# First attention of a four-stage kernel: q and k parts of each eight heads in their own 64 partitions and DRAM block, with row 0 written and loaded per block and its low parts made on VectorE

## The chip, the cores and the metric

One core of a Trainium2 chip. The metric is the device time of one execution in microseconds (us), median of several runs; the profile is of one execution of its own.

## What is computed

Four residual blocks run one after the other on x of shape (4, 1024, 128): an attention with a window of 64 keys, a gated linear attention with routing, an attention mixed with a recurrent state, and a mixture of experts. The change touches the first block alone:

```python
def _L0_attn_ref(x, Wq, Wk, Wv, Wo):          # x: layer-normed, 16 heads of 8 values
    q = (x @ Wq.T).reshape(b, s, 16, 8)
    k = (x @ Wk.T).reshape(b, s, 16, 8)
    v = (x @ Wv.T).reshape(b, s, 16, 8)
    attn = jnp.einsum('bqhd,bkhd->bhqk', q, k) / np.sqrt(8)
    allowed = (j <= i) & (j > i - 64)
    attn = softmax(jnp.where(allowed, attn, -jnp.inf))
    out = jnp.einsum('bhqk,bkhd->bqhd', attn, v).reshape(b, s, 128)
    return out @ Wo.T
x = x + _L0_attn_ref(_layernorm(x), ...)
```

## The kernel before, in words

A "row" is one of the four batch rows (b = 0 to 3) of 1024 positions. `window()` is the first attention. Every engine walks one list, `window_order()`, and does its own share of each item in that order; semaphores (named signals, `wait_ge`) join them. So an engine that waits in an item holds all its later items back.

For each row: `norm`, `log`, `root`, `tiles`, `turn` make the normed row and transpose it; `q` and `k` project it (TensorE, L496) into PSUM (128 partitions x 1024). To score in bf16 without losing the fp32 result, q and k are each split into three bf16 parts: the high part (ScalarE, L679), the rest in fp32 (VectorE, L612), the mid part (ScalarE, L684), and the low part (GpSimd, L828, `pool_low`). These parts lie in SBUF (`a_parts`), with one copy for q and one for k, so a row's parts may be made only when the row before has been read out.

SyncE writes the parts to DRAM (`a_scratch`, L748): each of the three parts goes to one, two or three of the six places of a stack (`PLACES`), 768, 512 and 256 KB for q, and the same sum for k in four DMAs. Then they are loaded back (L732, `load_half`) as stacks of 48 = 6 x 8 rows: one load has the four heads of a unit half `r` and goes to partitions 0-47 (r = 0) or 64-111 (r = 1). A unit (b, e) is eight heads of a row; e = 0, 1. Its four loads (q and k, r = 0 and 1) are 384 KB each. The loads `L` are issued by SyncE; those with r = 1 are issued by ScalarE (`L2`), but for unit (0, 0), where SyncE issues all four.

`M` (b, e, n) scores 128 queries for their maxima (TensorE, L475 the masks, L521 the products), and VectorE reduces them (L628). When the eight of a unit are done, GpSimd splits the negated maxima in three (L815 to L821), `S` transposes them (L530), ScalarE copies (L701), and SyncE puts them into rows 48-50 and 112-114 of the q stacks with six small DMAs (L763, the "shift rows"). `W` (b, e, m) then scores keys against queries (L475, L545), ScalarE exponentiates (L708), `V` weighs the values (L561), `D` and `E` add up (L718, L638). `M` items run seven ahead of `W`, which crosses units: in the list M(0,1,0) and M(0,1,1) stand ahead of S(0,0), and M(1,0,0) stands behind W(0,0,1).

At the start the list is: all of row 0's projection, its writes, `L` of (0,0), `L` of (0,1), values of row 0, norm and turn of row 1, `L2` of (0,1), `q` of row 1, M(0,0,0), `mid q` and `k` of row 1, three M, `mid k` of row 1, row 1's writes, four M, two M of (0,1), S(0,0), `L` of (1,0) and (1,1), `L2` of (1,0). Later rows' projections, writes and loads are spread over the steps of `W`: row 2's writes at steps 7 and 8, its first loads at 9, its first `L2` at 11; row 3 likewise 16 steps later.

Of the kernel before, what the change touches and what calls it, by code (L numbers as in the profile page):

```python
# [7 lines left out]
ALU = mybir.AluOpType  # L8
# [3 lines left out]
BF16 = mybir.dt.bfloat16  # L12

P = 128
BANK = 512
EPS = 1e-5
HEADS, HD = 16, 8
# [12 lines left out]
SPLIT = 3  # L30
# [85 lines left out]
def build(nc, x_in, packed, x_out, place, batches, T, known):  # L116
# [7 lines left out]
    with ctx:  # L124
# [7 lines left out]
        pe, dv, ac, gp, sp = (Queue(e) for e in (nc.tensor, nc.vector, nc.scalar, nc.gpsimd, nc.sync))  # L132
# [201 lines left out]
        a_scratch = {s: nc.dram_tensor(f"a_scratch_{s}", (batches, len(PARTS), P, T + P), BF16, kind="Internal").ap() for s in "qk"}  # L334
# [19 lines left out]
        def window_order():  # L354
# [7 lines left out]
                                 [("turn", b, 1)], [("q", b)], [("mid", b, "q"), ("k", b)], [("mid", b, "k")]]  # L362
# [16 lines left out]
            order = (flat(project(0)) + writes(0) + loads(0, 0) + loads(0, 1) + [("v", 0, 0), ("v", 0, 1)] + flat(second[:5])  # L379
# [43 lines left out]
        def window():  # L423
            s = "a"
# [165 lines left out]
            def dve_program():  # L590
                for ps in slots:
                    nc.vector.memset(ps[:, :], 0.0).then_inc(a_sums_cleared.up("all"), 1)
                for item in order:
# [13 lines left out]
                    elif kind in ("q", "k"):  # L607
                        b = item[1]
                        dv.wait_ge(a_split, (kind, b, "high"))
                        if b:  # L610
                            dv.wait_ge(a_low_made, (kind, b - 1))
                        nc.vector.tensor_tensor(a_rest[kind][:, :], ps[:, :], a_parts[kind][:, 0, :], ALU.subtract).then_inc(  # L612
                            a_rest_made.up((kind, b)), 1)
                    elif kind == "v":
# [46 lines left out]
            def act_program():  # L661
                for item in order:
# [11 lines left out]
                    elif kind in ("q", "k"):  # L674
                        b = item[1]
                        ac.wait_ge(a_projected, (kind, b))
                        if b:
                            ac.wait_ge(a_scratch_there[kind], b - 1)
# [7 lines left out]
                    elif kind == "L2":  # L686
# [4 lines left out]
                        ac.wait_ge(a_scratch_there[side], b)  # L691
# [38 lines left out]
            def load_half(engine, b, side, e, r):  # L730
                rows = a_scratch[side][b].rearrange("i (d r e p) t -> r e (i d) p t", r=2, e=2, d=HD)
                return engine.dma_start(a_stacks[side][b % 2][half(r, SCORE), SIDES * e:SIDES * (e + 1), :],  # L732
                                        rows[r, e][:, :, 0:T])

            def sp_program():
                for item in order:
                    kind = item[0]
                    if kind == "write":
                        _, b, side = item
                        for a in range(SPLIT):  # L740
                            if a < 2:
                                sp.wait_ge(a_split, (side, b, ("high", "mid")[a]))
                            else:
                                sp.wait_ge(a_low_made, (side, b))
                            for first, n, apart in PLACES[side][a]:
                                blocks = a_scratch[side][b].rearrange("i x t -> x i t")[
                                    :, first:first + (n - 1) * apart + 1:apart, 0:T]
                                nc.sync.dma_start(blocks, a_parts[side][:, a, :].unsqueeze(1).to_broadcast([P, n, T])).then_inc(  # L748
                                    a_scratch_there[side].up(b, 16), 16)
                    elif kind == "late":  # L750
                        sp_load_constants_late(a_staged)
                        for b in range(3, batches):
                            sp_load_x(b)
                        sp_load("b")
                    elif kind == "S":
                        _, b, e = item
                        u = unit(b, e)
                        sp.wait_ge(a_neg_T_made, (b, e))
                        for r in range(2):
                            for a in range(SPLIT):  # L760
                                row = 64 * r + SCORE + a
                                first = (r * SPLIT + a) * SIDES
                                nc.sync.dma_start(a_stacks["q"][b % 2][row:row + 1, SIDES * e:SIDES * (e + 1), :],  # L763
                                                  a_neg_T[u % 2][first:first + SIDES, :]).then_inc(
                                    a_shift_there[u % 2].up((b, e), 16), 16)
                    elif kind == "L":
                        _, b, side, e = item
                        sp.wait_ge(a_cleared, ("shift", b % 2))
                        if b >= 2:
                            sp.wait_ge(a_key_scored, ("W", b - 2, e, NT - 1))  # L770
                        sp.wait_ge(a_scratch_there[side], b)
                        for r in range(2 if (b, e) == (0, 0) else 1):
                            load_half(nc.sync, b, side, e, r).then_inc(stack_there[b % 2, e].up((s, b, e), 16), 16)
                        if item == ("L", 0, "k", 1):
                            sp_load_x(2)

            def pool_program():
# [13 lines left out]
                for side in "qk":  # L791
                    pool_low(side, 0)
# [30 lines left out]
            def pool_low(side, b):  # L823
                gp.wait_ge(a_split, (side, b, "mid"))
                gp.wait_ge(a_rest_made, (side, b))
                if b:
                    gp.wait_ge(a_scratch_there[side], b - 1)
# [1198 lines left out]
        def gla_first_pool():  # L2026

            gp.wait_ge(constants_made, "all")
            for side in "qk":
                gp.wait_ge(a_scratch_there[side], batches - 1)  # L2030
# [831 lines left out]
def weight_columns(i):  # L2862
# [11 lines left out]

    by_part = np.arange(P).reshape(-1, 2, HD).transpose(2, 1, 0).reshape(-1)
# [14 lines left out]
    for h in range(2):  # L2890
# [6 lines left out]
        "a_wq": i["L0_attn_Wq"].T[:, by_part], "a_wk": i["L0_attn_Wk"].T[:, by_part], "a_wv": i["L0_attn_Wv"].T,  # L2897
# [41 lines left out]
```

## Time and profile before

| | |
|---|---|
| median of 3 runs | 1802.07 us (1801.25 to 1804.1) |
| the profiled execution | 1806.19 us |
| its span, first to last instruction | 1804.9 us |
| mean granted TensorE clock | 0.951 of 2.4 GHz |
| busy: TensorE / VectorE / ScalarE / GpSimd | 1556.2 / 1275.3 / 1098.3 / 697.8 us |

The first attention fills about the first 280 us. A timeline row gives the start and the length in us, engine, line, operation, what it writes and reads, the count, and in brackets the idle time ahead of it and what ended that. SPq and ACTq are DMA issues of SyncE and ScalarE; a row of several goes from the first issue to the last and has their waits in it. "issue" as the releaser means that the profile shows nothing that the engine waited for.

### The profile page before, as it was taken

Reading aid. Unit: us, or ns where it says so; the run is one execution under the profiler, and the core shown is the slowest. Engines: PE = TensorE matmul, PEld = TensorE weight load, DVE = VectorE, ACT = ScalarE, POOL = GpSimd, SP = SyncE. Lnnn points to the kernel's source line nnn. Section 1 sums busy time; section 2 is a strip of 40 time slices with the busy share of each in tenths; the row PEclk is TensorE's granted clock in tenths of the full one; section 3 lists DMA queues with packets and bytes.
Section 4 is the critical chain, followed back from the end, with each engine's and each line's share of the span. In section 5 each row is a group of like instructions: output and inputs, shape, how many; then the busy total and the mean of one; then the engine's idle time right before and its main releaser. Section 6 shows DMA issues by size and latency. Waiting matters only on the chain. (4 is left out here: it accounts for less than half of the span.)

```text
span 1804.9 us, 45554 instructions
## 1 busy us (share of the span) xinstructions
PE 1556.2 (86%) x19648; PEld 998.5 (55%) x19648; DVE 1275.3 (71%) x2003; ACT 1098.3 (61%) x1641; POOL 697.8 (39%) x499
## 2 busy tenths in 40 slices
PE   3587897899999999999977778888788888899999
PEld 2354566787778778877863232433333343466565
DVE  4656644777777677768767868778777886655665
ACT  3255576777767777786752567677667767533331
POOL 4122300554255344534450556365465545411100
PEclk8789898999999999999997889999999999999999
DMA  7864200000000000000024274246237222223332
GB/s 176 196 165 113 47 5 12 2 2 2 2 2 2 2 1 2 2 1 2 32 88 99 52 212 98 63 133 142 56 107 167 66 64 72 67 71 94 95 96 76
DMA packets 54821, 121.17 MB, mean 67 GB/s; under 512 B 6124, under 2 KB 14468, under 8 KB 53020
## 3 DMA queue, kind: packets, MB, share of 16 engines
q1 hardware_dynamic: 51708, 112.74, 23.7%
q10 hardware_dynamic: 2912, 5.51, 1.8%
q8 instruction: 155, 2.54, 0.6%
q14 instruction: 46, 0.38, 0.1%
HBM read 85.70 MB, written 31.74 MB: 65 GB/s over the span
## 5 line engine op out<-in xcount | busy, mean ns | idle before, releaser
L1445 DVE TENSOR_REDUCE arena<-ring 128x2 f32<-128x1024 f32 (+2 forms) x320 | 342.1, 1110 | 87.9 <-PE ring L1302 62.1
L1545 ACT ACTIVATE arena<-ring 128x1024 f32<-128x1024 f32 (+1 forms) x320 | 291.3, 937 | 135.4 <-PE ring L1331 92.0
L1352 PE MATMUL accs<-arena 128*9 128x512 f32 (+3 forms) x1536 | 174.3, 528 | 3.8 <-ACT arena L1545 3.8
L2509 POOL TENSOR_TENSOR arena<-arena 128x1280 f32<-128x1280 f32 x28 | 65.3, 2332 | 287.0 <-PE accs L2270 231.7
L1295 PE MATMUL ring<-arena 48*128 48x512 bf16 (+3 forms) x768 | 128.8, 347 | 41.8 <-DVE arena L1445 21.1
L1324 PE MATMUL ring<-arena 51*128 51x512 bf16 (+3 forms) x768 | 125.0, 343 | 45.8 <-DVE arena L1445 25.1
L2501 POOL TENSOR_TENSOR arena<-arena 128x512 f32<-128x512 f32 x112 | 141.3, 1294 | 3.0 <-DVE arena L2311 3.0
L287 POOL TENSOR_SCALAR xn<-x,moments,rstd 128x128 f32<-128x128 f32 x80 | 65.0, 825 | 192.3 <-DVE rstd L258 178.3
L2782 ACT ACTIVATE arena<-ring 128x512 f32<-128x512 f32 x80 | 47.7, 596 | 134.8 <-PE ring L2651 132.7
L2494 POOL TENSOR_TENSOR arena<-arena 128x1024 f32<-128x1024 f32 x32 | 86.3, 2698 | 108.1 <-DVE arena L2368 108.1
L1718 POOL TENSOR_TENSOR arena<-arena 128x1024 f32<-128x1024 f32 x28 | 65.9, 2354 | 128.6 <-ACT arena L1558 104.5
L2742 DVE TENSOR_TENSOR arena<-arena,ring 128x512 f32<-128x512 f32 x80 | 54.9, 687 | 82.9 <-PE ring L2653 70.3
L1324 PEld LDWEIGHTS ring<-arena 51*128 51x128 bf16 x768 | 36.6, 95 | 137.9 <-DVE arena L1445 75.6
L2665 PEld LDWEIGHTS accs<-weights_large,arena 128*128 128x128 f32 x640 | 83.6, 193 | 37.9 <-issue 31.6
L1295 PEld LDWEIGHTS ring<-arena 48*128 48x128 bf16 x768 | 38.4, 96 | 110.3 <-DVE arena L1445 42.6
L2665 PE MATMUL accs<-weights_large,arena 128*128 128x128 f32 x640 | 85.3, 277 | 0.7 <-DVE arena L2748 0.7
L2454 ACT ACTIVATE arena<-arena 128x512 f32<-128x512 f32 x128 | 81.4, 707 | 0.0
L628 DVE TENSOR_REDUCE arena<-ring 128x8 f32<-128x1024 f32 x49 | 59.3, 1220 | 29.2 <-PE ring L521 29.0
L2246 PE MATMUL ring<-arena 128*64 128x256 f32 x512 | 76.0, 381 | 0.0
L1706 POOL TENSOR_TENSOR arena<-arena 128x1024 f32<-128x1024 f32 x32 | 75.5, 2360 | 0.1
L1455 DVE TENSOR_TENSOR_SCAN arena<-arena 128x1024 f32<-128x1024 f32 x32 | 73.8, 2306 | 2.3 <-POOL arena L1706 2.3
L2244 PEld LDWEIGHTS ring<-arena 128*64 128x64 f32 x512 | 36.1, 135 | 60.2 <-issue 30.6
(342 smaller groups left out, 4165.9 us busy)
## 6 DMA issues: line engine op xcount, KB each, us to landing
arena<-whole_k SPq DMA_DIRECT2D x32, 512.0 KB, 4.6
arena<-whole_q SPq DMA_DIRECT2D x32, 512.0 KB, 6.2
arena<-moe_scratch SPq DMA_DIRECT2D x128, 128.0 KB, 2.9
arena<-c_scratch_q SPq DMA_DIRECT2D x14, 384.0 KB, 9.3
arena<-c_scratch_k SPq DMA_DIRECT2D x14, 384.0 KB, 12.2
a_scratch_k<-arena SPq DMA_DIRECT2D x8, 512.0 KB, 4.2
c_scratch_k<-arena SPq DMA_DIRECT2D x8, 512.0 KB, 4.5
arena<-a_scratch_q SPq DMA_DIRECT2D x9, 384.0 KB, 7.2
```

Source lines behind the costliest of these rows:

```text
L1295: mm = nc.tensor.matmul(o[r], qs[half(r, SCORE), pair, n * P:(n + 1) * P], ks[half(r, SCORE), pair, a:c], start=True, stop=not diag)
L1324: mm = nc.tensor.matmul(o[r], ks[half(r, SHIFT), 2 * g + pair, j * P:(j + 1) * P], qs[half(r, SHIFT), 2 * g + pair, a:a + cols], start=Tru ...
L1352: mm = nc.tensor.matmul(acc[ci % 2][32 * h:32 * h + HD + 1, a - c * BANK:BANK], c_values[b % 2][:, j, r * HEADS // 2 + 2 * g + i, :], weig ...
L1445: nc.vector.tensor_reduce(dst, src, AX.X, ALU.max, negate=True).then_inc(c_max_taken.up(item), 1)
L1455: nc.vector.tensor_tensor_scan(sk[:, :], c_retain[:, j:j + 1].to_broadcast([P, T]), sk[:, :], 0.0, ALU.mult, ALU.add).then_inc(c_state_mad ...
L1545: nc.scalar.activation(view(c_probs[wi % 4]), view(ps), ACT.Exp).then_inc(c_weights_made.up(item), 1)
L1706: nc.gpsimd.tensor_tensor(sk[:, :], sk[:, :], c_vT[:, :], ALU.mult).then_inc(c_kv_made.up((b, j)), 1)
L2246: mm = nc.tensor.matmul(ps[r * GLA_D:(r + 1) * GLA_D, o + GLA_D:o + DENSE * GLA_D], k_nat[1][:, cols], v5[t % 2][:, 1:DENSE, cols], start= ...
L2454: nc.scalar.activation(v5[t % 2][:, 1 + r, :], v5[t % 2][:, 0, :], ACT.Copy, scale=route_hot[t // NT % 2][:, t % NT, r:r + 1]).then_inc(v_ ...
L2494: nc.gpsimd.tensor_tensor(masked[0][:, :], masked[0][:, :], masked[1][:, :], ALU.add).then_inc(gla_joined.up(t), 1)
L2501: nc.gpsimd.tensor_tensor(pair_cols(q2m[:, r, :]), pair_cols(q2[t % 2][:, :]), hot_b[t % 2][:, r * P:(r + 1) * P].unsqueeze(1).to_broadcas ...
L2665: mm = nc.tensor.matmul(moe_total(b, h)[:, n * P:(n + 1) * P], hid[i % 3][:, n * P:(n + 1) * P], w("d_down", f * P, (f + 1) * P), start=f ...
```

## The change

The columns of the q and k weights are permuted (`by_eights`), so that the heads of unit half e lie in partitions 64e to 64e + 63 of the projection, and the DRAM scratch has a block for each e. Each write DMA becomes two, one for each e, of 64 partitions and half the bytes: 14 for a row where there were 7. For row 0, SyncE writes the seven of e = 0, issues the four loads of (0,0), writes the seven of e = 1, and issues the loads of (0,1). For later rows all writes stand together, and every load waits for both blocks (`(b, 1)`). `k` of row 0 stands ahead of `mid q`, and row 0's two low parts move from GpSimd to VectorE. Each line that waits for `a_scratch_there` of a row as a whole waits for `(b, 1)`.

```diff
-        a_scratch = {s: nc.dram_tensor(f"a_scratch_{s}", (batches, len(PARTS), P, T + P), ...) for s in "qk"}
+        a_scratch = {s: nc.dram_tensor(f"a_scratch_{s}", (batches, 2, len(PARTS), P // 2, T + P), ...) for s in "qk"}
...
-                                 [("turn", b, 1)], [("q", b)], [("mid", b, "q"), ("k", b)], [("mid", b, "k")]]
+                                 [("turn", b, 1)], [("q", b)], [("mid", b, "q"), ("k", b)] if b else [("k", b), ("mid", b, "q")], [("mid", b, "k")]]
...
-            order = (flat(project(0)) + writes(0) + loads(0, 0) + loads(0, 1) + ...
+            order = (flat(project(0)) + [("write first", 0, 0)] + loads(0, 0) + [("write first", 0, 1)] + loads(0, 1) + ...
...
+                    elif kind == "mid" and item[1] == 0:
+                        side = item[2]
+                        dv.wait_ge(a_split, (side, 0, "mid"))
+                        dv.wait_ge(a_rest_made, (side, 0))
+                        nc.vector.tensor_tensor(a_parts[side][:, 2, :], a_rest[side][:, :], a_parts[side][:, 1, :],
+                                                ALU.subtract).then_inc(a_low_made.up((side, 0)), 1)
...
                         if b:
-                            ac.wait_ge(a_scratch_there[kind], b - 1)
+                            ac.wait_ge(a_scratch_there[kind], (b - 1, 1))
                         nc.scalar.activation(a_parts[kind][:, 0, :], ps[:, :], ACT.Copy).then_inc(
...
-                        ac.wait_ge(a_scratch_there[side], b)
+                        ac.wait_ge(a_scratch_there[side], (b, 1))
                         load_half(nc.scalar, b, side, e, 1).then_inc(a_second_there[b % 2, e].up((b, e), 16), 16)
...
+            def sp_write(b, side, e, a):
+                if a < 2:
+                    sp.wait_ge(a_split, (side, b, ("high", "mid")[a]))
+                else:
+                    sp.wait_ge(a_low_made, (side, b))
+                for first, n, apart in PLACES[side][a]:
+                    blocks = a_scratch[side][b, e].rearrange("i x t -> x i t")[
+                        :, first:first + (n - 1) * apart + 1:apart, 0:T]
+                    nc.sync.dma_start(blocks, a_parts[side][half(e, P // 2), a, :].unsqueeze(1).to_broadcast([P // 2, n, T])).then_inc(
+                        a_scratch_there[side].up((b, e), 16), 16)
...
                     if kind == "write":
                         _, b, side = item
+                        for e in range(2):
+                            for a in range(SPLIT):
+                                sp_write(b, side, e, a)
+                    elif kind == "write first":
                         for a in range(SPLIT):
+                            for side in "qk":
+                                sp_write(0, side, item[2], a)
...
-                        sp.wait_ge(a_scratch_there[side], b)
+                        sp.wait_ge(a_scratch_there[side], (b, e if b == 0 else 1))
...
-                for side in "qk":
-                    pool_low(side, 0)
...
+    by_eights = np.arange(P).reshape(2, -1, 2, HD).transpose(0, 3, 2, 1).reshape(-1)
...
-        "a_wq": i["L0_attn_Wq"].T[:, by_part], "a_wk": i["L0_attn_Wk"].T[:, by_part], ...
+        "a_wq": i["L0_attn_Wq"].T[:, by_eights], "a_wk": i["L0_attn_Wk"].T[:, by_eights], ...
```

SyncE's queue at the start, before: row 0's writes, then the loads of (0,0) and (0,1).

```order
L748 DMA a_scratch_q<-arena 128x3x1024 [waits a_split]
L748 DMA a_scratch_q<-arena 128x2x1024 [waits a_split]
L748 DMA a_scratch_q<-arena 128x1024 [waits a_low_made]
L748 DMA a_scratch_k<-arena 128x2x1024 [waits a_split]
L748 DMA a_scratch_k<-arena 128x1024
L748 DMA a_scratch_k<-arena 128x2x1024 [waits a_split]
L748 DMA a_scratch_k<-arena 128x1024 [waits a_low_made]
L732 DMA arena<-a_scratch_q 48x4x1024 [waits a_scratch_there_q,a_cleared]
L732 DMA arena<-a_scratch_q 48x4x1024
L732 DMA arena<-a_scratch_k 48x4x1024 [waits a_scratch_there_k]
L732 DMA arena<-a_scratch_k 48x4x1024
L732 DMA arena<-a_scratch_q 48x4x1024
```

And now, from the first load of (0,0) on (seven writes of 64 partitions stand ahead of it):

```order
L738 DMA arena<-a_scratch_q 48x4x1024 [waits a_scratch_there_q,a_cleared]
L738 DMA arena<-a_scratch_q 48x4x1024
L738 DMA arena<-a_scratch_k 48x4x1024 [waits a_scratch_there_k]
L738 DMA arena<-a_scratch_k 48x4x1024
L749 DMA a_scratch_q<-arena 64x3x1024
L749 DMA a_scratch_k<-arena 64x2x1024
L749 DMA a_scratch_k<-arena 64x1024
L749 DMA a_scratch_q<-arena 64x2x1024
L749 DMA a_scratch_k<-arena 64x2x1024
L749 DMA a_scratch_q<-arena 64x1024
L749 DMA a_scratch_k<-arena 64x1024
L738 DMA arena<-a_scratch_q 48x4x1024 [waits a_scratch_there_q]
```

Seven writes now stand between the loads of (0,0) and those of (0,1).

ScalarE, in the changed kernel, from row 1's turned tiles on: the two loads are `L2` of (0,1), the next row is the high part of row 1's q.

```order
L299 ACTIVATE xnT<-accs 128x512 [waits xn_turned]
L738 DMA arena<-a_scratch_q 48x4x1024 [waits a_scratch_there_q,a_cleared]
L738 DMA arena<-a_scratch_k 48x4x1024 [waits a_scratch_there_k]
L685 ACTIVATE arena<-ring 128x1024 [waits a_projected]
L690 ACTIVATE arena<-arena 128x1024 [waits a_rest_made]
L685 ACTIVATE arena<-ring 128x1024 [waits a_projected]
```

The rows stand as they did; what `a_scratch_there` is waited for has moved behind the loads of (0,0).

VectorE at the same places, the difference: the two low parts of row 0, and then row 1's rest of q ahead of the first reduction of (0,0).

```order
 L612 TENSOR_TENSOR arena<-accs,arena 128x1024
-L619 COPY arena<-ring 128x64x8 x2
+L618 TENSOR_TENSOR arena<-arena 128x1024 x2
+L625 COPY arena<-ring 128x64x8 x2
...
 L612 TENSOR_TENSOR arena<-ring,arena 128x1024
-L628 TENSOR_REDUCE arena<-ring 128x8
+L634 TENSOR_REDUCE arena<-ring 128x8
 L612 TENSOR_TENSOR arena<-ring,arena 128x1024
```

Two subtractions are new there; the reductions keep their place behind L612 of row 1.

## Rows read from the trace of the kernel before

**Rows 1.** The page: busy time, and 40 slices of 45.1 us (tenths).
```profile
PE 1556.2 (86%) x19648; PEld 998.5 (55%) x19648; DVE 1275.3 (71%) x2003; ACT 1098.3 (61%) x1641; POOL 697.8 (39%) x499
PE   3587897899999999999977778888788888899999
DMA  7864200000000000000024274246237222223332
```

**Rows 2.** Timeline, row 0's parts, writes and first loads.
```profile
17.60 6.35 SPq L748 DMA_DIRECT2D a_scratch_q<-arena  x3
18.86 1.06 ACT L684 ACTIVATE arena<-arena 128x1024 bf16<-128x1024 f32 x1 [1.29 <-DVE arena L612]
19.82 1.01 ACT L679 ACTIVATE arena<-accs 128x1024 bf16<-128x1024 f32 x1
20.86 1.23 DVE L612 TENSOR_TENSOR arena<-accs,arena 128x1024 f32<-128x1024 f32 x1 [2.04 <-ACT arena L679]
21.46 4.21 POOL L828 TENSOR_TENSOR arena<-arena 128x1024 bf16<-128x1024 f32 x2
23.99 2.74 SPq L748 DMA_DIRECT2D a_scratch_k<-arena  x4
...
30.12 0.79 SPq L732 DMA_DIRECT2D arena<-a_scratch_k  x2
```

**Rows 3.** Stretches (last three columns: PE clock, DMA share, GB/s moved).
```profile
24.50:29.00 4.50, 0.56 (x3) 0.50 (x3) 3.50 (x19) 0.51 (x2) 1.17 (x1) 0.60 1.03 380
30.00:37.00 7.00, 3.26 (x7) 1.28 (x6) 1.31 (x2) 2.97 (x4) 0.26 (x1) 0.74 1.08 173
41.00:44.00 3.00, 2.32 (x22) 1.45 (x23) 1.21 (x1) 0.00 (x0) 0.00 (x0) 0.50 1.07 251
```

**Rows 4.** DMA issues from 17 to 24 us (KB, us from issue to landing).
```profile
a_scratch_q<-arena SPq DMA_DIRECT2D x1, 256.0 KB, 2.0
```

**Rows 5.** Timeline, row 1's q and k beside the first scores.
```profile
33.30 1.02 ACT L679 ACTIVATE arena<-ring 128x1024 bf16<-128x1024 f32 x1 [2.04 <-PE ring L496]
...
41.68 0.64 PE L475 MATMUL ring<-bf_win_first,ident 64*64 64x512 bf16 x2 [8.42 <-DMA arena<-a_scratch_k]
...
42.79 1.23 DVE L628 TENSOR_REDUCE arena<-ring 128x8 f32<-128x1024 f32 x1 [7.21 <-PE ring L521]
...
48.45 1.22 DVE L628 TENSOR_REDUCE arena<-accs 128x8 f32<-128x1024 f32 x1
```

**Rows 6.** Timeline: second loads of (1,0), shift rows, first W, first M of (1,0).
```profile
59.46 0.46 ACTq L732 DMA_DIRECT2D arena<-a_scratch_k  x1
60.09 3.89 SPq L763 DMA_DIRECT2D arena<-arena  x6
...
64.51 0.73 SPq L732 DMA_DIRECT2D arena<-a_scratch_k  x1
...
68.61 0.64 PE L475 MATMUL ring<-bf_win_col,ident 64*64 64x512 bf16 x4 [5.38 <-DMA arena<-arena]
...
73.06 0.64 PE L475 MATMUL ring<-bf_win_first,ident 64*64 64x512 bf16 x2 [2.52 <-issue]
```

**Rows 7.** DMA issues from 64.45 to 65.2 us.
```profile
arena<-a_scratch_k SPq DMA_DIRECT2D x1, 384.0 KB, 8.5
```

**Rows 8.** Timeline, row 2: SyncE's writes, ScalarE's loads and what follows them.
```profile
98.84 6.56 SPq L748 DMA_DIRECT2D a_scratch_q<-arena  x3
105.44 3.56 SPq L748 DMA_DIRECT2D a_scratch_k<-arena  x4
...
113.73 0.36 ACTq L732 DMA_DIRECT2D arena<-a_scratch_k  x1
114.14 0.42 ACT L216 ACTIVATE bf_half_rows<-arena 128x256 bf16<-128x256 f32 x1 [0.77 <-DMA a_scratch_k<-arena]
```

**Rows 9.** Timeline, row 3: the same.
```profile
162.70 5.16 SPq L748 DMA_DIRECT2D a_scratch_k<-arena  x4
...
171.60 0.71 ACTq L732 DMA_DIRECT2D arena<-a_scratch_k  x1
```

**Rows 10.** Waits of TensorE from 60 to 190 us (us in total, times, longest).
```profile
PE ring L561 <- issue: 8.6, 2, 7.0
...
PE ring L586 <- issue: 3.8, 1, 3.8
```

More of the change, by code:

```diff
@@ L332, in build @@
         a_staged = carve([P, sizes["s"] + sizes["t"]])
-        a_scratch = {s: nc.dram_tensor(f"a_scratch_{s}", (batches, len(PARTS), P, T + P), BF16, kind="Internal").ap() for s in "qk"}
+        a_scratch = {s: nc.dram_tensor(f"a_scratch_{s}", (batches, 2, len(PARTS), P // 2, T + P), BF16, kind="Internal").ap() for s in "qk"}
         a_cleared, a_sums_cleared = signal("a_cleared"), signal("a_sums_cleared")
@@ L378, in window_order @@
             second, rows = project(1), maxima(units[0])
-            order = (flat(project(0)) + writes(0) + loads(0, 0) + loads(0, 1) + [("v", 0, 0), ("v", 0, 1)] + flat(second[:5])
+            order = (flat(project(0)) + [("write first", 0, 0)] + loads(0, 0) + [("write first", 0, 1)] + loads(0, 1) + [("v", 0, 0), ("v", 0, 1)] + flat(second[:5])
                      + seconds(0, 1) + second[5] + rows[0:1] + second[6] + rows[1:4] + second[7] + writes(1) + rows[4:]
@@ L730, in load_half @@
             def load_half(engine, b, side, e, r):
-                rows = a_scratch[side][b].rearrange("i (d r e p) t -> r e (i d) p t", r=2, e=2, d=HD)
+                rows = a_scratch[side][b, e].rearrange("i (d r p) t -> r (i d) p t", r=2, d=HD)
                 return engine.dma_start(a_stacks[side][b % 2][half(r, SCORE), SIDES * e:SIDES * (e + 1), :],
-                                        rows[r, e][:, :, 0:T])
+                                        rows[r][:, :, 0:T])
+            def sp_write(b, side, e, a):
[8 more added lines that the diff above has]
+                        a_scratch_there[side].up((b, e), 16), 16)
             def sp_program():
@@ L739, in sp_program @@
                         _, b, side = item
+                        for e in range(2):
+                            for a in range(SPLIT):
+                                sp_write(b, side, e, a)
+                    elif kind == "write first":
                         for a in range(SPLIT):
[L741 to L749, printed above, removed]
+                            for side in "qk":
+                                sp_write(0, side, item[2], a)
                     elif kind == "late":
@@ L826, in pool_low @@
                 if b:
-                    gp.wait_ge(a_scratch_there[side], b - 1)
+                    gp.wait_ge(a_scratch_there[side], (b - 1, 1))
                 nc.gpsimd.tensor_tensor(a_parts[side][:, 2, :], a_rest[side][:, :], a_parts[side][:, 1, :],
@@ L2029, in gla_first_pool @@
             for side in "qk":
-                gp.wait_ge(a_scratch_there[side], batches - 1)
+                gp.wait_ge(a_scratch_there[side], (batches - 1, 1))
             for t in (*w_T, *hot_T, *hot1_T):
@@ L2896, in weight_columns @@
     return {
-        "a_wq": i["L0_attn_Wq"].T[:, by_part], "a_wk": i["L0_attn_Wk"].T[:, by_part], "a_wv": i["L0_attn_Wv"].T,
+        "a_wq": i["L0_attn_Wq"].T[:, by_eights], "a_wk": i["L0_attn_Wk"].T[:, by_eights], "a_wv": i["L0_attn_Wv"].T,
         "a_wo": i["L0_attn_Wo"].T[by_eight],
```

## The prediction

> **What bounds the kernel now.** I read the page first, then the timeline of the first 75 us, then stretches with their DMA rate, then rows 2 and 3 of the attention. TensorE is busy 86% of the span, but only about three tenths in the first slice and five in the second, where the DMA engines are at seven and eight tenths [rows 1]. So the start is bound by transfers, and the change acts there. Row 0's parts are made by 26 us, and TensorE's first scores begin at 41.68 after 8.42 us of waiting for the k loads [rows 5]. Two things fill the time between: GpSimd's low parts end at 25.67, and the k loads are issued at 30.12, when all k writes have landed [rows 2]; then the loads themselves move at 173 GB/s, while the writes before them moved at 380 [rows 3]. The writes read 128 partitions, a load writes 48 within one half. This difference decides my forecast.
>
> The first scores are not the only gate. VectorE takes row 1's rest of q ahead of the first reduction, and that needs ScalarE's high part of q, which stands behind `L2` of (0,1). Before, that high part was made at 33.30, hidden under the wait for the loads; the first reduction ran at 42.79, the second at 48.45 [rows 5]. Afterwards come the shift rows, which let the first W start at 68.61, and the first M of (1,0) at 73.06, which is when the k load issued at 64.51 lands, 8.5 us later [rows 6, 7].
>
> **The change, part by part.** A row's writes are 12 blocks (six places, q and k) x 128 rows x 2048 bytes = 3.15 MB; one e is 1.57 MB, as are a unit's four loads.
>
> *Rate of a 64-partition write.* No row has one. Its bounds are 173 GB/s (48 partitions of one half, a load) and 380 (128 partitions, a write) [rows 3]. The load moved 0.46 of the rate with 0.38 of the partitions, so the rate goes roughly with the partitions; I take half of 380, 190 GB/s. Then one e takes 8.3 us and a row 16.6, where a row took 8.3. The Trainium skill, SBUF — State Buffer, section on the DMA port swizzle, speaks against such a change: partitions 0 to 63 reach half of the ports, 196 GB/s against 328 for all 128. By its figure a row's writes would be 16.1 us, an estimate; no row here shows a 64-partition write.
>
> *Landing.* 256 KB landed 2.0 us after its issue [rows 4], of which 0.7 is data at 380: I add 1.3 after the last byte.
>
> *Low parts on VectorE.* k's high part follows q's at once (1.01), then q's rest, k's rest (1.23), the mid parts (1.06 each), two subtractions like L612 (1.23): the last low part is ready at about 23.0 instead of 25.67 [rows 2]. But seven writes of e = 0, begun at 17.9, need 8.3 us and end at 26.2, so the earlier low part buys nothing at 190 GB/s. What VectorE does behind (values, norm of row 1) moves by some 1 us and has cover: row 1's high q is late for another reason.
>
> *First loads.* They start at 27.5 (landing), take 1.57/173 = 9.1 us, and land at 37.9: TensorE's first scores 3.8 us **earlier** than 41.68.
>
> *Second writes and what waits for them.* They stand behind the loads in SyncE's queue: 36.6 to 44.9, landed 46.2. There ScalarE sits in `L2` of (0,1), and its high q follows at 46.5 instead of 33.30. Then in a chain: high q 47.5, rest 48.8, mid q 49.8, high k 50.8, rest k 52.1. The second reduction starts at 52.1 instead of 48.45, **3.6 later**. The first scores' gain is lost on VectorE.
>
> *Row 1.* Loads of (0,1), both halves at once from two queues, at the 251 GB/s of such a stretch [rows 3]: 6.3 us, to 52.5. The Trainium skill, same page, section "Can I just issue two DMAs to hit both halves?", gives only 6% for two transfers in different halves; the row has 251 against 173, 45%, and the measurement decides. By the rule these loads would end 2.3 us later and the sum would be 2.3 higher. Then 0.52 MB of x (1.4 us), then row 1's writes 16.6 us: to 70.5, landed 71.8. The shift rows queue behind them, so the first W is at 71.8 instead of 68.61 (+3.2). The last k load of (1,0) waits for the writes too: behind q's 0.39 MB it ends at 70.5 + 0.79/173 = 75.1, landed 76.4 instead of 73.06. **+3.3** for all before 76 us.
>
> *Rows 2 and 3.* When q's last part is issued, at 105.06 of the 98.84 + 6.56 group [rows 8], there are left 0.13 MB of it, 0.79 of q's e = 1 and 1.57 of k: 2.49 MB, 13.1 us at 190, so k lands at 119.8. ScalarE's k load, at 113.73, had already waited 0.77 us for this landing [rows 8]: **+6.1**, in ScalarE's queue, which holds the exponentials of every step. Row 3: from 162.6, just ahead of k's group, the same 13.1 us end at 177.0 with landing, against 171.60 [rows 9]: **+5.4**. One exponential's worth (1 us) in each is covered by the scores already in PSUM: +5.1 and +4.4.
>
> *A give-back.* Just after those loads TensorE stood 3.84 and 7.0 us with "issue" as the releaser [rows 10], while both DMA queues were full. In the new kernel q's loads run while ScalarE waits for k, so about half of the loading is over when TensorE goes on. I take half of 10.8 back: **-5.4**. Bounds: 0 and -10.8.
>
> *Issues.* 28 more write DMAs on SyncE at some 0.4 us stand behind waits or ahead of a full queue: nothing. Two low parts off GpSimd: it waited for TensorE's work anyway. The permuted columns cost nothing, being packed before the launch.
>
> Sum: 3.3 + 5.1 + 4.4 - 5.4 = +7.4 us. Nothing behind 200 us has changed, and TensorE's eight or nine tenths there take the delay through to the end. The profiled execution would go from 1806.2 to 1813.6; the median of the runs shown is 4.1 below it, so I forecast 1802.1 + 7.4 = **1809.5 us**.
>
> **Rivals.**
> *B, given back whole.* All 10.8 us of the TensorE waits vanish: 12.8 - 10.8 = +2.0, 1804. For: they occur only where both queues load. Against: slower writes leave the queues full for longer, and new waits may come.
> *C, writes at 380 from 64 partitions.* The limit in rows 3 would be one of loads (writing SBUF) alone. Then low k at 23.0 sets the end: first block landed 25.1, loads to 34.9, second block landed 40.3, the second reduction at 46.2, 2.2 earlier; rows 2 and 3 as before: 1800. For: no row shows a read from one half. Against: nothing else than the partitions explains 173.
> *D, the other side: the first scores' gain goes through.* The second block's writes overlap with the loads of (0,0), since one reads and the other writes SBUF and the queue runs on 16 engines that finish apart. If they land by 39.0 us, the second reduction (5.9 us behind) starts by 44.9, over 3.6 earlier; with full overlap and 380 GB/s, -4.6: 1797.5. Later than 40, nothing is gained beyond C. Against: the same queue moved nothing ahead of its turn in row 0 before.
>
> **How the numbers follow.** A measurement can tell about 0.2%, 3.6 us. The forecast's own range, with writes from 220 down to 173 GB/s and the give-back from all to none, is 1804 to 1820. Chances: A 0.64 (I count it slower; its tail below 3.6 is B's), B 0.10, C 0.16 (a quarter of it over 3.6 faster), D 0.10. Faster 0.14, same 0.22, slower 0.64. The range 1797.5 to 1820 leaves out the worst of A and the best of D.
>
> **What would show it.** Right: a stretch of row 1's or 2's writes at about 190 GB/s; first scores near 38 us; the high part of row 1's q near 46.5, with ScalarE idle ahead of it; the second reduction near 52; the first M of (1,0) near 76; ScalarE 5 to 6 us in the k load of rows 2 and 3. Wrong: writes above 300 GB/s (C), the second block landed before 40 (D), no idle in ScalarE at rows 2 and 3, or "issue" waits of TensorE gone or grown.

## The result, and the profile after

| | before | after |
|---|---|---|
| median of 6 runs | 1800.53 us (1797.6 to 1804.1) | 1813.02 us (1811.51 to 1818.04) |
| the profiled execution | 1806.19 us | 1811.91 us |
| its span | 1804.9 us | 1810.6 us |
| mean granted TensorE clock | 0.951 | 0.947 |

The change makes the kernel slower: the ratio is 1.0074, interval 1.0056 to 1.0092, and the medians differ by 12.5 us. The six runs of before include the three of the table ahead. Here and below a median counts every execution, while a ratio leaves out the few that were far off, such as one of spread's twelve (1890.91 us at a granted clock of 0.818). The profiled executions differ by 5.7 us only, because that of before lies 5.7 us above its own median. This turns out to matter.

The page of after, the lines of [rows 1]:

```profile
PE 1561.8 (86%) x19648; PEld 1003.1 (55%) x19648; DVE 1277.6 (71%) x2005; ACT 1098.6 (61%) x1641; POOL 694.4 (38%) x497
...
PE   3678898899999999999987778888788888899999
...
DMA  6965400000000000000024173246237222223232
```

The second, fourth and fifth slices have more DMA than before: half writes keep the engines occupied for longer.

The timeline of after from 17 to 49 us, which answers to [rows 2] and [rows 5]:

```profile
17.41 0.71 SPq L749 DMA_DIRECT2D a_scratch_q<-arena  x1
...
20.28 2.43 DVE L618 TENSOR_TENSOR arena<-arena 128x1024 bf16<-128x1024 f32 x2
...
27.44 0.93 SPq L738 DMA_DIRECT2D arena<-a_scratch_k  x2
28.41 0.61 SPq L749 DMA_DIRECT2D a_scratch_q<-arena  x1
...
32.32 0.60 SPq L749 DMA_DIRECT2D a_scratch_k<-arena  x1
...
38.86 0.63 PE L475 MATMUL ring<-bf_win_first,ident 64*64 64x512 bf16 x2 [5.17 <-DMA arena<-a_scratch_k]
...
43.05 1.02 ACT L685 ACTIVATE arena<-ring 128x1024 bf16<-128x1024 f32 x1 [11.17 <-DMA a_scratch_k<-arena]
44.11 1.22 DVE L612 TENSOR_TENSOR arena<-ring,arena 128x1024 f32<-128x1024 f32 x1 [13.40 <-ACT arena L685]
...
45.25 1.21 DVE L634 TENSOR_REDUCE arena<-ring 128x8 f32<-128x1024 f32 x1
...
48.51 1.21 DVE L634 TENSOR_REDUCE arena<-accs 128x8 f32<-128x1024 f32 x1
```

The low parts end at 22.7 (25.67 before), the k loads are issued at 27.44 (30.12) and the first scores start at 38.86 (41.68). Then ScalarE stands 11.17 us in `L2` of (0,1), row 1's high q comes at 43.05 instead of 33.30, and VectorE's rest of q behind it holds the reductions. The second one is at 48.51, 0.06 us from where it was.

Stretches of after, as [rows 3]: the writes of e = 0, the loads of (0,0), the writes of e = 1, row 1's writes, row 2's writes:

```profile
19.00:26.00 7.00, 0.82 (x8) 0.63 (x6) 6.69 (x16) 3.39 (x4) 1.71 (x2) 0.73 0.93 199
28.50:37.00 8.50, 4.62 (x12) 2.48 (x12) 2.17 (x9) 1.20 (x2) 0.00 (x0) 0.70 1.09 168
38.50:41.50 3.00, 2.64 (x22) 1.48 (x23) 0.00 (x0) 0.00 (x0) 0.00 (x0) 0.50 0.96 366
...
55.00:59.00 4.00, 1.77 (x28) 1.35 (x20) 3.77 (x4) 0.00 (x0) 1.12 (x4) 0.50 1.04 386
111.00:114.00 3.00, 3.00 (x130) 1.92 (x128) 2.40 (x5) 2.83 (x5) 0.94 (x1) 1.00 0.95 205
```

The same kind of write, 64 partitions of one half, runs at 199 and 205 GB/s in two places and at 366 and 386 in two others. The engines are busy 93 to 104% in all four.

The timeline of after at the starts of (1,0), row 2 and row 3, which answers to [rows 6], [rows 8] and [rows 9]:

```profile
60.80 4.06 SPq L777 DMA_DIRECT2D arena<-arena  x6
...
66.34 0.48 PE L475 MATMUL ring<-bf_win_col,ident 64*64 64x512 bf16 x4 [2.96 <-DMA arena<-arena]
...
75.39 0.64 PE L475 MATMUL ring<-bf_win_first,ident 64*64 64x512 bf16 x2 [7.29 <-DMA arena<-a_scratch_k]
...
102.14 9.84 SPq L749 DMA_DIRECT2D a_scratch_q<-arena  x6
...
112.03 7.51 SPq L749 DMA_DIRECT2D a_scratch_k<-arena  x8
...
123.38 0.32 ACTq L738 DMA_DIRECT2D arena<-a_scratch_k  x1
123.74 0.42 ACT L216 ACTIVATE bf_half_rows<-arena 128x256 bf16<-128x256 f32 x1 [6.93 <-DMA a_scratch_k<-arena]
...
126.14 0.64 PE L475 MATMUL accs<-bf_win_col,ident 64*64 64x512 bf16 x4 [6.79 <-ACT arena L714]
...
184.59 1.02 ACT L714 ACTIVATE arena<-ring 128x1024 f32<-128x1024 f32 x1 [6.21 <-DMA a_scratch_k<-arena]
```

The first M of (1,0) is at 75.39 (73.06 before). In rows 2 and 3 ScalarE waits 6.93 and 6.21 us for k's writes; before it waited 0.77 in row 2 [rows 8]. TensorE takes 6.79 us of the first over. From the first q write of row 2 to ScalarE's k load it is 21.2 us (102.14 to 123.38), where it was 14.9 (98.84 to 113.73).

Waits of TensorE from 60 to 190 us, which answer to [rows 10]:

```profile
PE accs L475 <- ACT arena L714: 6.8, 1, 6.8
...
PE ring L561 <- issue: 1.9, 1, 1.9
...
PE ring L586 <- issue: 0.7, 1, 0.7
```

The 7.0 and 3.8 us with "issue" are gone. The forecast counted half of that as a gain.

### The profile page after: what moved, and what is told of

Same layout as the page of the kernel before. It is cut to its first block and busy times, and to the rows that moved or that the text cites. A ratio compares the mean times of both kernels' runs of the same rounds, so it can differ in the third digit from the quotient of the medians.

```text
span 1810.6 us, 45583 instructions
## 1 busy us (share of the span) xinstructions
PE 1561.8 (86%) x19648; PEld 1003.1 (55%) x19648; DVE 1277.6 (71%) x2005; ACT 1098.6 (61%) x1641; POOL 694.4 (38%) x497
## 5 line engine op out<-in xcount | busy, mean ns | idle before, releaser
L2754 DVE TENSOR_TENSOR arena<-arena,ring 128x512 f32<-128x512 f32 x80 | 54.9, 687 | 84.8 <-PE ring L2665 72.2
L2677 PEld LDWEIGHTS accs<-weights_large,arena 128*128 128x128 f32 x640 | 84.0, 193 | 38.5 <-issue 32.7
L714 ACT ACTIVATE arena<-ring 128x1024 f32<-128x1024 f32 x46 | 46.9, 1020 | 41.5 <-PE ring L545 34.6
```

Source lines behind the costliest of these rows:

```text
L2677: mm = nc.tensor.matmul(moe_total(b, h)[:, n * P:(n + 1) * P], hid[i % 3][:, n * P:(n + 1) * P], w("d_down", f * P, (f + 1) * P), start=f ...
```

## The experiments

The theory: the half writes of rows 1 to 3 make the loss, through the wait of ScalarE in `L2`. Its rivals: the loss is that of row 0's split; or it is where `L2` stands; or the writes' order and number matter and not their rate. Eleven runs follow, of nine changed kernels: before_again is one more execution of before, and low_only_again is low_only timed again. All but before_again were timed beside before on the same chip, where before's median was 1801.4 to 1802.4 us; against these the change is some 11 us slower, against its own six runs 12.5.

**before_again**: no edit, a second profiled execution of before.

> The kernel before, profiled once more, to see whether the two TensorE waits of 7.0 and 3.84 us with "issue" as releaser (rows 10) belong to it or to that one execution. If they belong to it, they stand again at 112 to 126 and 176 to 184 us, and W of row 3 ends near 273 us again. If they are noise of one execution, they are gone or elsewhere, the span is some 5 us shorter (near 1799), and the give-back in my sum had nothing to give back.

Measured: 1799.29 us, span 1797.9, 7.0 below the first profiled execution. Waits of TensorE from 60 to 280 us:

```profile
PE ring L586 <- issue: 3.2, 1, 3.2
PE ring L561 <- issue: 2.9, 2, 1.8
PE ring L475 <- issue: 2.5, 1, 2.5
```

The 7.0 us wait at L561 of [rows 10] isn't there; it doesn't come in every execution. It isn't a freak of one either: whole_later, below, has 6.46 us at the same place. The 3.8 us wait at L586 is there, with 3.2 us, and after has only 0.7. So of the 10.8 us that the forecast could give back, some 3 stand in both executions of before. As this execution lies 1.2 us below the median of before and the first one 5.7 above, it is the better one to lay beside after, and it is used so below.

**whole_later**: row 0 as in the change; rows 1 to 3 with the old columns, the old scratch and seven writes of 128 partitions.

```diff
-                    mm = nc.tensor.matmul(ps[...], w(f"a_w{kind}"),
+                    mm = nc.tensor.matmul(ps[...], w(f"a_w{kind}" + ("2" if b else "")),
...
+                    if b:
+                        blocks = a_scratch_whole[side][b].rearrange("i x t -> x i t")[...]
+                        nc.sync.dma_start(blocks, a_parts[side][:, a, :].unsqueeze(1).to_broadcast([P, n, T])).then_inc(
+                            a_scratch_there[side].up((b, 1), 16), 16)
```

> The change for row 0 alone; rows 1 to 3 keep the old permutation (two more weight tables), the old scratch and whole 128-partition writes. Theory 1 (slow half writes of rows 1 to 3 hold ScalarE's L2 and the loads): the first M of (1,0) goes back from 75.4 to about 71 us, ScalarE's waits of 6.9 and 6.2 us at rows 2 and 3 are under 1 us, and the time is at or 2 us below before: 1798 to 1801. Rival (row 0's new order is what costs): it stays near 1810.

Measured: 1802.84 us, ratio 1.0011 (0.9994 to 1.0028). From row 2's first q write to ScalarE's k load it is 14.4 us again (99.58 to 113.96), and ScalarE doesn't wait for k's writes. The loss sits in the later rows' writes; row 0's split costs or brings nothing that this measurement can tell. The long wait of [rows 10] is back in this execution:

```profile
182.66 1.04 PE L562 MATMUL ring<-arena 64*9 64x128 f32 x24 [6.46 <-issue]
```

**alternate**: the same half writes, each part's two halves behind each other instead of all of e = 0 first.

```diff
-                        for e in range(2):
-                            for a in range(SPLIT):
+                        for a in range(SPLIT):
+                            for e in range(2):
                                 sp_write(b, side, e, a)
```

> The change with the write DMAs of rows 1 to 3 in another order: high e=0, high e=1, mid e=0, mid e=1, low e=0, low e=1; bytes, partitions and number the same. If what costs is that the high and mid parts of e=1 stand behind the low part of e=0 on SyncE, ScalarE's k load of row 2 goes back by about 5 us (it then has 0.5 MB less than half of the 2.5 MB to wait for) and the time falls to about 1804. If it is the rate of 64-partition writes alone, the queue never runs dry either way and little changes: 1811 to 1814.

Measured: 1803.54 us, ratio 1.0004 (0.9988 to 1.0019). The same DMAs in another order take back nearly all of the loss. Row 2 of its timeline:

```profile
98.06 7.77 SPq L749 DMA_DIRECT2D a_scratch_q<-arena  x6
105.89 6.67 SPq L749 DMA_DIRECT2D a_scratch_k<-arena  x8
...
116.89 0.42 ACT L216 ACTIVATE bf_half_rows<-arena 128x256 bf16<-128x256 f32 x1 [4.25 <-DMA a_scratch_k<-arena]
```

In the change the high and mid parts of e = 1 stand behind the wait for the low part of e = 0, which GpSimd makes last; here they go out while it is made. The stretch from the first write to ScalarE's k load falls from 21.2 to 18.4 us (98.06 to 116.48), still 3.5 above before. ScalarE still waits 4.25 us here and 5.60 in row 3, and yet the time is within 0.2% of before. Part of the gain lies ahead of these waits: row 1's writes go in the new order too, and row 2's begin at 98.06 instead of 102.14.

**late_seconds**: the change, with `L2` of rows 2 and 3 three steps later.

```diff
-                    side[at + NT + 3] += seconds(b + 2, 0)
+                    side[at + NT + 6] += seconds(b + 2, 0)
```

> The change with ScalarE's second loads of rows 2 and 3 three steps later in the list, nothing else. If their cost is that ScalarE, which holds every step's exponential, sits in a wait for slow writes, both waits of 6 to 7 us vanish and the time falls by 8 to 12 us, to 1801 to 1805, with writes as slow as before. Rival (what is late is the stack for M of (2,0) and (3,0)): the wait moves to TensorE and the time stays or rises.

Measured: 1815.56 us, ratio 1.0071 (1.0045 to 1.0097), as the change. ScalarE's waits are gone, and TensorE has them instead, for the stacks of (1,0), (2,0) and (3,0) (waits of TensorE from 60 to 280 us):

```profile
PE ring L475 <- DMA arena<-a_scratch_k: 19.1, 3, 9.1
```

The wait at (1,0) is in after too, with 7.29 us. So the wait of ScalarE can't be moved away at a gain. The run doesn't clear the place of `L2` of all blame, since `L2` issues half of each stack: its k loads now go out at 125.60 and 190.41 us, 2.1 and 3.9 behind SyncE's own, so the edit also makes the stacks of (2,0) and (3,0) later.

**row0_together**: the change, with row 0's fourteen writes together ahead of all loads.

```diff
-... [("write first", 0, 0)] + loads(0, 0) + [("write first", 0, 1)] + loads(0, 1) + ...
+... [("write first", 0, 0), ("write first", 0, 1)] + loads(0, 0) + loads(0, 1) + ...
-                        sp.wait_ge(a_scratch_there[side], (b, e if b == 0 else 1))
+                        sp.wait_ge(a_scratch_there[side], (b, 1))
```

> The change with row 0's fourteen half writes together and its loads behind them, so no load stands between the blocks of e=0 and e=1. In the changed kernel the second block went at about 366 GB/s right behind the loads (38.5 to 41.5 us) and the first at 199 (19 to 26). If a half write is slow whenever the 16 DMA engines run in step, as after an idle queue, and fast when unequal loads ahead have set them apart, the second block is slow here too: both end near 35 us at about 200 GB/s and the first scores start near 46. If the second half's partitions or a full queue make it fast, its writes go near 370 and end near 31, first scores near 41. Time: 1814 to 1818 by the first, 1808 to 1813 by the second.

Measured: 1816.78 us, ratio 1.008 (1.0049 to 1.0111). The first scores start at 49.59, 10.7 us later than in the change, and the first W at 77.05 instead of 66.34. The expectation had 46 for the first; the time fits its first case. The end moves by only 3.8 us (medians). Two stretches of it, both of half writes with no load ahead, the second with those of e = 1:

```profile
21.00:24.00 3.00, 0.00 (x0) 0.00 (x0) 3.00 (x5) 2.34 (x2) 0.18 (x1) 0.86 0.93 200
28.00:34.00 6.00, 4.24 (x12) 2.48 (x12) 2.82 (x12) 1.52 (x4) 0.00 (x0) 0.55 0.92 215
```

The writes of e = 1 go at 215 GB/s here and at 366 in the change, where loads of 48 partitions ran ahead of them. What changed is what was in the queue before. The packets of the trace show the two rates: the median packet of 2048 bytes takes 153 ns in after from 19 to 26 and from 111 to 114 us, and 147 here, but 84 in after from 38.5 to 41.5 and from 55 to 59, as with the whole writes of before (85 ns from 24.5 to 29).

**low_only**: before, with row 0's low parts on VectorE and `k` ahead of `mid q`; no half writes.

```diff
-... [("q", b)], [("mid", b, "q"), ("k", b)], [("mid", b, "k")]]
+... [("q", b)], [("mid", b, "q"), ("k", b)] if b else [("k", b), ("mid", b, "q")], [("mid", b, "k")]]
...
+                    elif kind == "mid" and item[1] == 0:
+                        side = item[2]
...
+                        nc.vector.tensor_tensor(a_parts[side][:, 2, :], a_rest[side][:, :], a_parts[side][:, 1, :],
...
-                for side in "qk":
-                    pool_low(side, 0)
```

> The kernel before with one part of the change: row 0's low parts on VectorE, and k ahead of mid q. Writes of 128 partitions, order and permutation stay. My terms: the last low part at 23 instead of 25.7 us, so k's last write is issued some 2.5 us earlier; the first loads start some 2 us earlier, the first scores near 39.5, first M of (1,0) at most 2 us earlier than 73. Time 0 to 2.5 us below before, inside what can be told. Rival (low parts in the same queue position were hidden behind the writes' own 8 us): no row moves by over 1 us.

Measured: 1800.78 us, ratio 0.9982 (0.9964 to 1.0001). Its first scores start at 38.92, as early as in the change (38.86), and the first M of (1,0) at 70.65, 2.4 us earlier than before [rows 6]:

```profile
38.92 0.63 PE L475 MATMUL ring<-bf_win_first,ident 64*64 64x512 bf16 x2 [5.02 <-DMA arena<-a_scratch_k]
...
70.65 0.64 PE L475 MATMUL ring<-bf_win_first,ident 64*64 64x512 bf16 x2 [3.10 <-issue]
```

The early start is thus had from the low parts and the place of `k` alone, with whole writes. The split of the scratch adds nothing to it that the traces can tell: the same kernel has 39.62 in low_only_again, and the kernels with the change's row 0 have 38.05 to 39.93.

**low_only_again**: the same kernel, timed a second time.

> The version with the low parts on VectorE alone, timed once more beside those two, because its interval (0.9964 to 1.0001) leaves open whether it is faster than the kernel before. If its 2.4 us at the first M of (1,0) carry through, the ratio is again near 0.998 to 0.999; if it was chance, near 1.000.

Measured: 1800.82 us, ratio 0.9997 (0.9975 to 1.002). The two intervals overlap between 0.9975 and 1.0001: a gain of up to 0.25% is possible and not established.

**rows_first**: alternate, with three M of (0,0) ahead of row 1's q in the list.

```diff
-... + seconds(0, 1) + second[5] + rows[0:1] + second[6] + rows[1:4] + second[7] + ...
+... + seconds(0, 1) + rows[0:3] + second[5] + rows[3:4] + second[6] + second[7] + ...
```

> On the version with alternating halves: three M of (0,0) stand ahead of row 1's q in the list, so their reductions do not wait behind VectorE's rest of row 1's q. If that order is what lost the gain of the early first scores, the first reduction runs near 39.5 instead of 44 us and the unit's last one some 3 us earlier, W of (0,0) up to 3 us earlier. If the scratch of row 1 (its parts, writes and loads) sets the first M of (1,0) anyway, that M stays at 72 to 74 and the time does not fall: 1801 to 1804. If it passes through: 1798 to 1800.

Measured: 1803.93 us, ratio 1.0005 (0.9988 to 1.0022), as alternate. The first reductions no longer wait for row 1's q, and the shift rows are issued at 57.76 instead of alternate's 59.33:

```profile
39.52 3.49 DVE L634 TENSOR_REDUCE arena<-ring 128x8 f32<-128x1024 f32 x3 [8.79 <-PE ring L521]
...
57.76 4.41 SPq L777 DMA_DIRECT2D arena<-arena  x6
```

The first M of (1,0) is at 72.83 all the same (72.10 in alternate), after a wait of 4.55 us for the k load. VectorE's order was a gate, but not the last.

**alternate_late1**: alternate, with `L2` of rows 2 and 3 one step later (`NT + 4`).

> Alternating halves, and ScalarE's second loads of rows 2 and 3 one step later. ScalarE waited 3 to 6 us in them with alternating halves. If one step (some 3 us) covers that without making the stacks late for M of (2,0) and (3,0), the time falls by 3 to 6 us, to 1798 to 1801. If the stacks are then late, as with three steps, TensorE waits there for the k load instead and the time is the same or higher.

Measured: 1806.51 us, ratio 1.0018 (1.0 to 1.0037). Of ScalarE's waits for k's writes 0.76 us is left in row 2 and none over 0.7 in row 3, and there is no gain, as with late_seconds.

**spread**: the change, with each e on every second partition instead of in one half of them.

```diff
-                    nc.sync.dma_start(blocks, a_parts[side][half(e, P // 2), a, :].unsqueeze(1)...
+                    nc.sync.dma_start(blocks, a_parts[side][e:P:2, a, :].unsqueeze(1)...
...
-    by_eights = np.arange(P).reshape(2, -1, 2, HD).transpose(0, 3, 2, 1).reshape(-1)
+    by_eights = np.arange(P).reshape(2, -1, 2, HD).transpose(3, 2, 1, 0).reshape(-1)
```

> The change with one thing different: the heads of e lie in every second partition (parity e) and not in one half, so a write DMA reads 64 partitions spread over all 128. Number, bytes and order of the DMAs are those of the change. If what halves the rate is that 64 partitions of one half are read, these go at 370 to 380 GB/s: first block landed near 25, first scores near 37, ScalarE's waits for the k loads of rows 2 and 3 gone, 1799 to 1802. If it is the number of partitions (or the smaller DMAs), the rate stays near 200 and the time near 1813.

Measured: 1805.3 us, ratio 1.0012 (0.9995 to 1.0029). Two stretches of it, row 0's writes of e = 0 and row 2's writes:

```profile
20.00:23.00 3.00, 1.68 (x15) 1.48 (x14) 2.21 (x3) 2.65 (x3) 1.44 (x2) 1.00 0.58 224
...
108.00:110.00 2.00, 2.00 (x104) 1.39 (x92) 1.60 (x3) 1.86 (x5) 0.51 (x1) 1.00 0.94 339
```

Row 2's writes reach 339 GB/s where the change had 205, at the same share of 0.94 or 0.95. The median packet takes 84 and 85 ns in the two stretches, where the change had 153. So the slow rate, where it comes, comes from reading 64 neighbouring partitions of one half. In row 0 the engines are busy 0.58 of the time only: the issues now set the pace. The stretch of row 2 from the first write to ScalarE's k load is 19.5 us (98.71 to 118.17): the rate alone gives back 1.8 of 6.3.

The expectation that ScalarE's waits would go was wrong: they are 6.12 and 6.52 us, about as long as in the change, and the time, over the 1799 to 1802 expected, is still 7.7 us below that of the change. So the length of these waits is no measure of the loss. What did move is the first M of (1,0), at 72.99 instead of 75.39, and that of (2,0), at 132.60 instead of 137.51.

**spread_alternate**: spread and alternate together.

> Spread partitions and alternating blocks for rows 1 to 3. With both repairs the scratch of rows 2 and 3 lands as in the kernel before (113 to 114 us for row 2); first M of (1,0) near 72; time 1797 to 1801 if the rate is repaired, near the alternating version's 1802 to 1804 if it isn't.

Measured: 1802.6 us, ratio 1.0002 (0.9983 to 1.002). Row 2 and the stretch of its writes:

```profile
98.27 7.45 SPq L749 DMA_DIRECT2D a_scratch_q<-arena  x6
105.78 6.80 SPq L749 DMA_DIRECT2D a_scratch_k<-arena  x8
...
117.55 0.42 ACT L216 ACTIVATE bf_half_rows<-arena 128x256 bf16<-128x256 f32 x1 [5.34 <-DMA a_scratch_k<-arena]
```

```profile
102.00:112.00 10.00, 7.96 (x301) 5.02 (x300) 6.88 (x8) 7.72 (x11) 4.54 (x3) 1.00 0.52 189
```

The two gains don't add up: it is 18.9 us to the k load (98.27 to 117.15). Rate and order are mended and four of the 6.3 us are still there. The issues run from 98.27 to 112.58, 14.3 us, where the seven whole writes took from 98.84 to 109.00, 10.2 us [rows 8], and the DMA engines stand idle for half of the stretch. It isn't that the low part came later. GpSimd makes k's here, and in before:

```profile
105.94 2.13 POOL L840 TENSOR_TENSOR arena<-arena 128x1024 bf16<-128x1024 f32 x1 [1.47 <-ACT arena L690]
```

```profile
106.50 2.14 POOL L828 TENSOR_TENSOR arena<-arena 128x1024 bf16<-128x1024 f32 x1 [1.47 <-ACT arena L684]
```

It is ready 9.8 us behind the first write in both. Before has one write left to issue then, this kernel four. So the 4 us of this stretch are the price of fourteen DMAs instead of seven in SyncE's queue; that is read from the traces, as no run changes the number alone. In the time of the kernel they can't be told (ratio 1.0002).

## Why the prediction was right, and where it was not

The sign, the range and the main mechanism held: 1813.0 lies in 1797.5 to 1820, above 1809.5, and case A, the forecast's own, came. Step by step, with before_again (which lacks the 7.0 us wait) beside after. First M of (2,0) and of (3,0), and the last W of the attention, in before_again:

```profile
129.15 0.38 PE L475 MATMUL ring<-bf_win_first,ident 64*64 64x512 bf16 x2
...
187.74 0.38 PE L475 MATMUL ring<-bf_win_first,ident 64*64 64x512 bf16 x2
...
263.35 0.41 PE L475 MATMUL ring<-bf_win_col,ident 64*64 64x512 bf16 x4
```

And in after:

```profile
137.51 0.38 PE L475 MATMUL ring<-bf_win_first,ident 64*64 64x512 bf16 x2
...
196.83 0.38 PE L475 MATMUL ring<-bf_win_first,ident 64*64 64x512 bf16 x2
...
273.01 0.41 PE L475 MATMUL ring<-bf_win_col,ident 64*64 64x512 bf16 x4
```

| stretch | term | measured |
|---|---|---|
| up to the first M of (1,0) | +3.3 | +2.2 (73.16 to 75.39) |
| from there to the first M of (2,0) | +5.1 | +6.1 (+8.4 in all) |
| from there to the first M of (3,0) | +4.4 | +0.7 (+9.1) |
| from there to the last W | 0 | +0.6 (+9.7) |
| from there to the end of the span | 0 | +3.0 (+12.7) |
| give-back | -5.4 | in the rows above |

One pair of executions is a rough scale. With whole writes in rows 1 to 3 (both executions of before, low_only twice, whole_later) the stretch from the first M of (1,0) to that of (2,0) took 55.6 to 59.3 us, and after's 62.1 is clear of it. The next stretch, to the first M of (3,0), took 54.9 to 61.9, and after's 59.3 is inside: of row 3's cost nothing is shown.

- **Low parts, first loads, first scores.** Right. Low parts at 22.7 (forecast 23.0), first scores at 38.86 (37.9). That the early low part buys nothing at 190 GB/s was right for the change; low_only and low_only_again show that with whole writes it buys 2.1 to 2.8 us.
- **Second writes and what waits for them.** The chain was right (`L2`, high q, rest of q, reduction), its size not: high q came at 43.05, not 46.5, since the block of e = 1 moved at 366 GB/s and not at 190. The second reduction was 0.06 us late, not 3.6. Rival D's condition (the block landed before 40) was missed, as row 1's high q at 43.05 shows, and the first scores' gain was lost on VectorE as forecast. rows_first shows that it would have been lost on row 1's scratch otherwise.
- **Row 1.** Its writes ran at 386 in the middle, so the first W came 2.3 us earlier than before instead of 3.2 later. The first M of (1,0) still was 2.2 late.
- **Rows 2 and 3.** ScalarE's waits were forecast as 5 to 6 us and measured 6.93 and 6.21. The cause was told wrongly: I had the rate alone, out of bytes left by 190 GB/s. By the stretch from row 2's first write to ScalarE's k load, the rate gives back 1.8 us alone, the order 2.8 alone, and some 4 us stay with the number of DMAs. The right size came out of a wrong split. Nor was it right to price the waits one for one: spread keeps 6.12 and 6.52 us of them and alternate 4.25 and 5.60, at 1.0012 and 1.0004, and the two runs that took them away gained nothing. In row 3 TensorE took only 3.31 us of ScalarE's wait, and its start slipped by 0.7. That the half writes of rows 1 to 3 make the loss, and that either another order or spread partitions take back most of it, is shown; which wait carries it to the end stays open. There is a slip in row 2's sum too: 119.8 counts from 105.40, the end of the q group, and from the 105.06 that it names it is 119.5, so the term is 4.7 and the sum +7.0.
- **Issues: "nothing".** This term failed. For row 2's writes it should have read some 4 us, from half writes that follow each other every 0.65 us (seven from 28.41 to 32.92) and not at 0.4, in a queue whose last write ScalarE waits for.
- **The give-back, -5.4.** The step that made the forecast too low. Two thirds of what it could give back is a wait that a second execution of the same kernel doesn't have. The other third is real: the wait at L586 is 3.2 us in before_again and 0.7 in after, so 2.5 us were given back. For the two profiled executions the forecast fits (+5.7 measured against +7.4); for the medians it doesn't. Without the term the sum is 12.8, the medians give 12.5. That agreement is partly luck, as the table shows: row 3 cost 3.7 less than its term, and 3.0 came behind the attention, where no term stood. That last stretch, span less last W, is 1534.6 us in before_again, 1537.6 in after, and 1534.4 to 1538.4 in the other traces, of kernels that are the same there, so I put it down to differences between executions; what makes them stays open.
- **Rival B** (all 10.8 given back) did not come as a time. Against the profiled execution nearly all of the two waits is gone, as it said, but new waits took their place (6.8 and 3.3 us of TensorE for ScalarE), and the 7.0 is not in every execution. **Rival C** (380 from 64 partitions) was right for two of the four stretches and wrong for row 0's e = 0 and for row 2. Its sum has a slip: from 25.1 the loads end at 34.2, not 34.9.

## What to carry to other kernels

Before a wait of a trace is counted as a gain or a loss, look whether a second execution of the same kernel has it; a wait with "issue" as its releaser above all. Here one of two came again and the other didn't. A wait that is new after a change is not yet the loss: look whether the time falls in a version that takes it away. If a DMA is cut in two, write the issuing queue down with its waits: each half costs its issue, and a half that stands behind a wait for the last part holds parts that have been ready for long. Find out which part of an edit brings the early start: here it was the two subtractions on VectorE with `k` ahead of `mid q`, not the split that they came with.

## What the runs showed of the hardware that I had not expected

- Writes from 64 neighbouring partitions have no single rate. They ran at 199 and 205 GB/s, 200 and 215 in row0_together, but at 366 and 386 behind loads of 48 partitions, at a busy share of 0.92 to 1.04 throughout. The Trainium skill, SBUF — State Buffer, in its section on the DMA port swizzle, gives partitions 0 to 63 half of the ports and 196 GB/s. The first four lie near it, the last two don't, and the measurement decides: from 38.5 to 41.5 us only writes of e = 1 were in the queue, so 366 GB/s came out of partitions 64 to 127 alone. A packet of 2048 bytes has a median of 147 or 153 ns in the first four and 84 in the last two. Why is open. That the engines go through the partitions in step, and that unequal loads ahead put them out of step, would fit; it is argued, not shown, as no run here changed the step alone.
- With every second partition instead of one half, the same writes reached 339 GB/s in row 2, where the change had 205. Behind the loads they had 393, where the change had 366 already:

```profile
37.00:40.00 3.00, 2.06 (x22) 1.06 (x23) 0.00 (x0) 0.00 (x0) 0.00 (x0) 0.80 1.04 393
```

- A half write costs 0.65 us of SyncE's queue where seven follow each other (28.41 to 32.92 in after), and this is what holds the writes back once the rate is mended: 0.52 busy share in row 2 of spread_alternate.
- The same kernel had 9.0 and 2.9 us of "issue" waits at L561 in two executions, and spans of 1804.9 and 1797.9 us; whole_later has 7.7 at that statement (its L562).
